# A perceiver layer: second-batch regrouping in its own buffer, most of it issued by SyncE, and the cross-attention's values one block sooner

## The chip, the cores and the metric

The kernel runs on one core of a Trainium2 chip. The metric is the device time of one execution in microseconds (us); the time before is the median of three runs, 1431.88 us (1429.88 to 1434.81). The engines are named as in the profile: PE (TensorE), ACT (ScalarE), DVE (VectorE), POOL (GpSimd) and SP (SyncE, which issues DMA transfers). ACT issues DMA transfers too; ACTq and SPq are the issues of the two.

## The reference

One layer of a perceiver, all in float32, for x of 2 x 256 tokens of width 256 and a context of 2 x 4096 tokens.

```python
x = x + xattn(layernorm(x), ctx, ctx)       # 16 heads of 64; softmax over 4096 keys
x = x + attn(layernorm(x))                  # self-attention, below
x = x + ffn(layernorm(x))                   # gated, weights in 4 bits, activations in 16

def attn(x):                                # k, v = 16 memory tokens + 256 own tokens
    dots = einsum('bhid,bhjd->bhij', q, k) * scale
    dots = einsum('bhij,hk->bkij', dots, pre_proj)      # heads are mixed ahead of the softmax
    dots = where(causal, finfo.min, dots)
    attn = softmax(dots)
    attn = einsum('bhij,hk->bkij', attn, post_proj)     # and behind it
    return (attn @ v) @ Wo
```

## The kernel before

Three stages follow one another: `cross_attention`, `self_attention`, `gated_ffn`. In each, every engine has a program of its own, written out by hand, and the engines meet by semaphores; an instruction waits for what is named ahead of it, and everything behind it on its engine waits too. The order of the lines is the order on the engine.

**Cross-attention.** 16 passes: 2 batches times 8 pairs of heads (`it` counts passes, `i` pairs in a batch). The 4096 keys are taken in 8 blocks of 512 (`STEPS`, index `j`). In the first half of a pass PE (`body`, L628) projects the keys of a block (`project_k`, L530) and, two blocks later, makes scores for the row maxima (`scores_for_max`, L559) in four score banks, which DVE reduces (L447) before the next block's scores overwrite them. Between them PE does what is left of the pass before (`sum_over_keys`, the denominators, after the scores of block 0; `project_output`, after those of block 2) and the value projections (`project_v`, L538): number j - 5 behind block j > 4, number 3 ahead of the last scores, 4 to 6 behind them, 7 after the transposes of the negated maxima (L655). DVE divides by the denominators (`divide`, L422) after the maxima of block 0 and adds the output to x (`add_output`, L430) after those of block 2. ACT copies keys and values out of the banks (`copy_v`, L352). Values alternate between two banks, `out_ps` (shared with denominators and output) and `v_ps` (shared with the queries); `v_bank` says which has the even ones. In the second half of a pass scores are made again, ACT takes exponentials, and PE multiplies by the values. In pair 0 of a batch each block has two value projections, one for each half of the keys.

**Self-attention.** Queries, keys and values are projected, and the dots of a pair of heads come out of PE with a query per partition. The head mix needs heads and 8 query rows together on the partitions (16 x 8 = 128), so the dots are regrouped by DMA from `dots_sb` to `grouped`: for each head one transfer for the near half (the first 128 queries, `t` = 0, 144 keys) and one for the far half (`t` = 1, 272 keys), each from 128 partitions to 8 (`send_dots`, L924). 16 heads, two halves and two batches make 64 transfers. Then 17 steps for each batch (`SA_STEPS`; n = 0 to 33) go through a pipeline: PE `mix(n)` (L1264), DVE mask and maximum, ACT exponentials, DVE reciprocals, POOL scales the second mixing matrix, PE `post(n - 3)` (L1277), DVE and ACT copy the result. Mix 0 and 17 wait for the near transfers of their batch, mix 8 and 25 for the far ones. Into the steps are woven: the transposes of the FFN's weights (steps 1 to 6, three banks in turn), the second batch's dots (`dots(PAIRS + u)`, steps 8 to 15, near and far of one pair at a time in one pair of banks), at step 20 the products of the first batch with its values (`all_products(0)`), and from step 22 its output projection.

The near and the far buffer of `grouped` exist once, for both batches. So SP and ACT send the second batch's near transfers only after 8 mixes are done, and the far ones after 17 (L953, L1082); SP sends the odd pairs of heads, ACT the even ones. A wait for the transfers of the memory values and of `v_last_b1` (the second batch's last 16 values, moved to the first partitions) stands ahead of mix 0 (L1352).

Of the kernel before, what the change touches and what calls it, by code (L numbers as in the profile page):

```python
# [12 lines left out]
P = 128  # L13
BATCH, SEQ, D = 2, 256, 256
# [63 lines left out]
def cross_attention(nc, x, ctx_in, w_q, w_k, w_v, w_o, x_res, ident):  # L78
# [16 lines left out]
    with ExitStack() as stack:  # L95
# [103 lines left out]
        def v_bank(m):  # L199
            return (out_ps, v_ps)[m % 2]  # L200
# [140 lines left out]
        def _(act):  # L341
# [20 lines left out]
            def body(it, b, i, parity):  # L362
# [5 lines left out]
                for j in range(STEPS + 1):  # L368
# [13 lines left out]
                    if j > 4:  # L382
                        copy_v(b, i, parity, j - 5)
                for j in range(STEPS - 4, STEPS - 1):
                    copy_v(b, i, parity, j)
# [32 lines left out]
        def _(dve):  # L418
# [17 lines left out]
            def body(it, b, i, parity):  # L436
# [7 lines left out]
                for j in range(STEPS):  # L444
# [4 lines left out]
                    if j == 0 and it > 0:  # L449
                        divide(it - 1)  # L450
# [43 lines left out]
        def _(pe):  # L494
# [43 lines left out]
            def project_v(it, b, i, parity, j):  # L538
# [89 lines left out]
            def body(it, b, i, parity):  # L628
                if not opened_before(it):
                    open_pair(it, b, i)  # L630
                for j in range(2, STEPS):
# [12 lines left out]
                    if j > 4:  # L644
# [5 lines left out]
                for j in range(STEPS - 4, STEPS - 1):  # L650
                    project_v(it, b, i, parity, j)
# [111 lines left out]
def self_attention(nc, w_q, w_kv, w_o, pre_proj, post_proj, mem_k, mem_v, w_gate, w_up, hidden_wT,  # L763
                   x_res, ident):

    with ExitStack() as stack:
# [26 lines left out]
        v_last_b1 = r.sbuf("v_last_b1", [MEM, INNER])  # L793
# [47 lines left out]
        dots_copied = [r.sem("dots_by_act"), r.sem("dots_by_dve")]  # L841
        regrouped = [r.sem("regrouped_near"), r.sem("regrouped_far")]
# [24 lines left out]
        def dots_bank(u):  # L867

            return pair_bank[u % 2 if u < PAIRS else 0]

        def hidden_bank(m):
            return bank[m % 3]
# [46 lines left out]
        DOTS_AT = SA_STEPS // 2  # L919
        HIDDEN_AT = 1  # L920
# [3 lines left out]
        def send_dots(eng, b, pair, t):  # L924

            for h in (2 * pair, 2 * pair + 1):
                eng.dma_start(grouped[t][h * ROWS:(h + 1) * ROWS, :, :], dots_sb[t][:, h, :]
# [5 lines left out]
        def _(sp):  # L933
# [16 lines left out]
            sp.dma_start(v_last_b1[:, :], v_last[MEM:2 * MEM, :]).then_inc(last_in, 16)  # L950
# [55 lines left out]
        def copy_dots(eng, scaled_copy, u):  # L1006

            pair = u % PAIRS
            eng.wait_ge(dots_made, u + 1)
            if u >= PAIRS:  # L1010
                for t in range(QT):
                    eng.wait_ge(regrouped[t], ALL_REGROUPED)
            src = dots_bank(u)
            scaled_copy(dots_sb[0][:, 2 * pair:2 * pair + 2, :], src[:, :, 0:NEAR])
            scaled_copy(dots_sb[1][:, 2 * pair:2 * pair + 2, :], src[:, :, NEAR:NEAR + KEYS]
                        ).then_inc(dots_copied[u % 2], 1)

        @block.scalar
        def _(act):
# [10 lines left out]
            def send(b, pair):  # L1030

                act.wait_ge(dots_copied[0], (b * PAIRS + pair) // 2 + 1)
                for t in range(QT):
                    send_dots(act, b, pair, t)
# [32 lines left out]
            for n in range(STEP_ALL + LAG):  # L1067
# [4 lines left out]
                if HIDDEN_AT <= n - 1 < HIDDEN_AT + 2 * WT_BANKS:  # L1072
                    m = n - 1 - HIDDEN_AT
                    act.wait_ge(hidden_made, m + 1)
                    copy(hidden_wT[:, m // WT_BANKS, m % WT_BANKS * 512:(m % WT_BANKS + 1) * 512], hidden_bank(m)
                         ).then_inc(hidden_copied, 1)
                u = n - DOTS_AT
                if 0 <= u < PAIRS and u % 2 == 0:
# [653 lines left out]
```

## Time and profile before

| | |
|---|---|
| median of 3 runs | 1431.88 us (1429.88 to 1434.81) |
| profiled execution | 1433.27 us, its span 1431.1 us |
| busy in the span | PE 1262.2 us (88%), DVE 877.0 (61%), ACT 723.9 (51%), POOL 412.6 (29%) |
| mean granted PE clock | 0.952 of full speed |
| cross-attention, self-attention, FFN | until about 1125, until about 1337, until 1431 |

All times in rows are microseconds from the start of the span. Busy time is the time of an engine's instructions, without its waits. A line of code can have several groups of instructions, as it makes different tiles. A row of a timeline has an instruction or a run of equal ones; in square brackets stands how long the engine had been idle before it, and what it then waited for.

### The profile page before, as it was taken

To read this page: it belongs to the slowest core of one execution; us is meant where nothing else is said; L and a number is where in the kernel's file an instruction comes from. 1 tells how busy PE (TensorE), PEld (TensorE's weight loads), DVE (VectorE), ACT (ScalarE), POOL (GpSimd) and SP (SyncE) were. 2 spreads that over 40 slices of the span, in tenths; PEclk is the share of its full clock that TensorE was granted. 3 is DMA by queue.
4 is the path that set the end of the run, shared out by engine and by line. 5 is a ranking of instruction groups with operands and counts; after the bars stand their busy time and mean duration, and the time that the engine had idled before them with its cause. 6 is when DMAs were issued, how large, how long until landed. Compare 5 with 4: busy or idle time off the path is not lost. (4 is left out here: it accounts for less than half of the span.)

```text
span 1431.1 us, 21060 instructions
## 1 busy us (share of the span) xinstructions
PE 1262.2 (88%) x8379; PEld 943.1 (66%) x8379; DVE 877.0 (61%) x1042; ACT 723.9 (51%) x1304; POOL 412.6 (29%) x372
## 2 busy tenths in 40 slices
PE   3999999999999999899999999999999697569643
PEld 2786877768686868586868687776868344346322
DVE  4647666676766676647676766667676456304476
ACT  3655656565555555545565565656554133214153
POOL 3605051432425150414251505143241103102000
PEclk9999999999999999999999999999999799859876
DMA  4203020203111132211121303030311442330000
GB/s 150 74 1 78 1 78 1 78 1 78 30 49 49 27 84 83 77 30 30 49 52 27 78 1 78 0 78 1 74 31 33 164 61 41 48 49 1 22 0 15
DMA packets 42528, 68.19 MB, mean 48 GB/s; under 512 B 5040, under 2 KB 31152, under 8 KB 42432
## 3 DMA queue, kind: packets, MB, share of 16 engines
q1 hardware_dynamic: 37632, 63.39, 17.1%
q10 hardware_dynamic: 4800, 3.48, 1.9%
q8 instruction: 66, 1.08, 0.3%
q14 instruction: 30, 0.25, 0.1%
HBM read 25.89 MB, written 0.52 MB: 18 GB/s over the span
## 5 line engine op out<-in xcount | busy, mean ns | idle before, releaser
L447 DVE TENSOR_REDUCE step_max<-score_banks 128x2 f32<-128x1024 f32 x256 | 299.0, 1220 | 124.3 <-PE score_banks L571 124.3
L468 DVE TENSOR_TENSOR prob_sum<-prob_sum,probs 128x1024 f32<-128x1024 f32 x224 | 279.3, 1288 | 139.6 <-ACT probs L398 138.9
L330 POOL TENSOR_TENSOR k_split<-probs,k_split 64x512 fp32r<-64x512 f32 x128 | 163.4, 1277 | 328.8 <-ACT probs L381 323.8
L398 ACT ACTIVATE probs<-score_banks 128x1024 f32<-128x1024 f32 x181 | 181.9, 1028 | 149.3 <-PE out_ps L597 85.3
L585 PE MATMUL score_banks<-q_twice,k_split 128*128 128x256 f32 x724 | 182.2, 288 | 0.2 <-ACT probs L398 0.2
L586 PE MATMUL score_banks<-q_low_max,k_ones 128*128 128x256 f32 x724 | 178.1, 283 | 0.0
L332 POOL TENSOR_TENSOR k_split<-probs,k_split 64x512 fp32r<-64x512 f32 x128 | 164.0, 1281 | 9.6
L585 PEld LDWEIGHTS score_banks<-q_twice,k_split 128*128 128x128 f32 x724 | 138.3, 191 | 11.9 <-issue 6.2
L323 POOL TENSOR_TENSOR w_lo<-w_raw,w_hi 128x768 fp32r<-128x768 f32 x16 | 36.2, 2261 | 355.5 <-ACT w_hi L349 355.5
L586 PEld LDWEIGHTS score_banks<-q_low_max,k_ones 128*128 128x128 f32 x724 | 138.5, 191 | 0.0
L373 ACT ACTIVATE k_split<-key_banks 64x512 fp32r<-64x512 f32 x128 | 75.6, 590 | 119.2 <-PE key_banks L534 118.6
L571 PE MATMUL score_banks<-k_split,q_twice 64*128 64x512 f32 x512 | 103.3, 461 | 27.9 <-DVE step_max L447 27.9
L597 PE MATMUL out_ps<-probs,v_near 128*64 128x256 f32 x1024 | 121.0, 383 | 0.4 <-ACT probs L398 0.4
L597 PE MATMUL out_ps<-probs,v_far 128*64 128x256 f32 x1024 | 120.9, 383 | 0.0
L398 ACT ACTIVATE probs<-key_banks 128x1024 f32<-128x1024 f32 x75 | 77.1, 1029 | 43.7 <-PE out_ps L597 42.9
L534 PE MATMUL key_banks<-ctxT_lo,w_hi 128*128 128x512 f32 x256 | 93.1, 445 | 2.6 <-ACT probs L381 1.4
L597 PEld LDWEIGHTS out_ps<-probs,v_near 128*64 128x64 f32 x1024 | 69.8, 137 | 38.8 <-issue 2.4
L597 PEld LDWEIGHTS out_ps<-probs,v_far 128*64 128x64 f32 x1024 | 69.9, 137 | 38.4 <-issue 2.9
L571 PEld LDWEIGHTS score_banks<-k_split,q_twice 64*128 64x128 f32 x512 | 42.4, 186 | 79.1 <-issue 30.5
L534 PE MATMUL key_banks<-ctxT_hi,w_lo 128*128 128x512 f32 x256 | 81.8, 401 | 0.0
L534 PE MATMUL key_banks<-ctxT_hi,w_hi 128*128 128x512 f32 x256 | 81.6, 400 | 0.0
L381 ACT ACTIVATE probs<-key_banks 128x512 f32<-128x512 f32 x128 | 76.7, 599 | 4.8 <-POOL k_split L332 1.7
(207 smaller groups left out, 2204.4 us busy)
## 6 DMA issues: line engine op xcount, KB each, us to landing
k_ones<-k_split SPq DMA_DIRECT2D x128, 256.0 KB, 4.0
ctx_rows<-in_ctx_dram SPq DMA_DIRECT2D x10, 512.0 KB, 3.8
w_raw<-in_L_xattn_w_v_dram SPq DMA_DIRECT2D x14, 256.0 KB, 3.5
probs<-in_ctx_dram SPq DMA_DIRECT2D x6, 512.0 KB, 6.2
grouped_far<-dots_far ACTq DMA_DIRECT2D x16, 136.0 KB
grouped_far<-dots_far SPq DMA_DIRECT2D x16, 136.0 KB
w_raw<-in_L_xattn_w_q_dram SPq DMA_DIRECT2D x16, 128.0 KB, 3.6
w_raw<-in_L_xattn_w_k_dram SPq DMA_DIRECT2D x16, 128.0 KB, 3.5
```

The lines of the kernel that those rows point to most:

```text
L330: pool.tensor_tensor(k_split[DH:P, A, keys], keys_staged[j % 2][0:DH], k_split[0:DH, A, keys].bitcast(F32), ALU.subtract).then_inc(k_low[A ...
L332: pool.tensor_tensor(k_split[0:DH, B, keys], keys_staged[j % 2][DH:P], k_split[DH:P, B, keys].bitcast(F32), ALU.subtract).then_inc(k_low[B ...
L373: act.activation(k_split[0:DH, A, keys], ps[0:DH, :], ACT.Copy).then_inc(k_high, 1)
L381: act.activation(keys_staged[j % 2], ps[:, :], ACT.Copy).then_inc(k_staged, 1)
L398: act.activation(probs[:, j % 2, h, :], scores_of, ACT.Exp, scale=SCALE).then_inc(exp_done, 1)
L447: dve.tensor_reduce(step_max[:, qt, :, j], score_banks[:, 2 * qt:2 * qt + 2, :], X, ALU.max).then_inc(max_done, 1)
L468: dve.tensor_tensor(prob_sum[:, h, :], prob_sum[:, h, :], probs[:, j % 2, h, :], ALU.add).then_inc(sum_done, 1)
L534: last = mm(k_ps[j % 2][:, :], w[:, c, 0:PAIR], s[:, c, j * CHUNK:(j + 1) * CHUNK], start=(n == 0), stop=(n == len(passes) - 1))
L571: last = mm(score_banks[:, 2 * qt + 1 - h, :], q_twice[rows, h, qt * P:(qt + 1) * P], k_split[rows, h, keys], start=True, stop=True)
L585: mm(out, k_split[:, h, keys], q_twice[:, h, :], start=True, stop=False)
L586: last = mm(out, k_ones[:, h, keys], q_low_max[:, h, :], start=False, stop=True)
L597: last = mm(out_ps[h * DH:(h + 1) * DH, SEQ:2 * SEQ], v[:, h * DH:(h + 1) * DH], probs[:, j % 2, h, t * SEQ:(t + 1) * SEQ], start=(j == 0 ...
```

## The change

Cross-attention:
- In pairs with i > 0 the value projections stand behind the blocks 3, 5, 6 and 7 (numbers 0 to 3), one is put ahead of the last scores (4) and two behind them (5, 6). In pair 0 of a batch they stay.
- Even values take `v_ps`, odd ones `out_ps`, and the two waits for these banks change places.
- DVE divides after the maxima of block 1 (before: block 0).

Self-attention:
- `grouped` has a near buffer for each batch; the far one is still shared. `v_last_b1` lies in `xnT`, which is no longer needed by then.
- The second batch's dots are split: the near ones of pair n are made in step n (0 to 7) in the first pair of banks, the far ones in steps 8 to 15 in the same banks. ACT and DVE copy them by turns, each at its own step; PE makes the next pair's when the last one's copy is done.
- The second batch's near transfers are issued by SP as soon as a pair is copied; its far ones all by SP, after 17 mixes. Of the first batch ACT issues the near transfers of even pairs, SP all others.
- The FFN's weight transposes stand in steps 1, 3, 5, 7, 9 and 11, in one bank.
- The waits for the memory values and `v_last_b1` go from ahead of mix 0 to the products of the first batch.

```diff
 # cross-attention
         def v_bank(m):
-            return (out_ps, v_ps)[m % 2]
+            return (v_ps, out_ps)[m % 2]
+        def values_behind(i, j):
+            return (j - 5 if j > 4 else None) if i == 0 else {3: 0, 5: 1, 6: 2, 7: 3}.get(j)
+        def values_left(i):
+            return list(range(3 if i == 0 else 4, STEPS - 1))
...
-                    if j == 0 and it > 0:
+                    if j == 1 and it > 0:
                         divide(it - 1)
...
                     if t == 0 and m == 0:
+                        pe.wait_ge(q_low, 2 * it + 2)
+                    elif t == 0 and m == 1:
                         wait_past(pe, y_added, it)
-                    elif t == 0 and m == 1:
-                        pe.wait_ge(q_low, 2 * it + 2)
...
-                    if j > 4:
-                        project_v(it, b, i, parity, j - 5)
+                    if values_behind(i, j) is not None:
+                        project_v(it, b, i, parity, values_behind(i, j))
                 scores_for_max(it, STEPS - 2)
-                project_v(it, b, i, parity, STEPS - 5)
+                project_v(it, b, i, parity, values_left(i)[0])
                 scores_for_max(it, STEPS - 1)
-                for j in range(STEPS - 4, STEPS - 1):
+                for j in values_left(i)[1:]:
                     project_v(it, b, i, parity, j)
 # self-attention: buffers and SP's program
-        grouped = [r.sbuf("grouped_near", [P, P // ROWS, NEAR]), r.sbuf("grouped_far", [P, P // ROWS, KEYS])]
+        near = [r.sbuf(f"grouped_near{b}", [P, P // ROWS, NEAR]) for b in range(BATCH)]
+        far = r.sbuf("grouped_far", [P, P // ROWS, KEYS])
+        grouped = [[near[b], far] for b in range(BATCH)]
...
-            for pair in range(1, PAIRS, 2):
-                sp.wait_ge(dots_copied[1], pair // 2 + 1)
-                for t in range(QT):
-                    send_dots(sp, 0, pair, t)
+            for pair in range(PAIRS):
+                sp.wait_ge(dots_copied[pair % 2], pair // 2 + 1)
+                if pair % 2 == 1:
+                    send_dots(sp, 0, pair, 0)
+                send_dots(sp, 0, pair, 1)
+            for pair in range(PAIRS):
+                sp.wait_ge(near_copied[pair % 2], pair // 2 + 1)
+                send_dots(sp, 1, pair, 0)
...
-            for t in range(QT):
-                sp.wait_ge(mix_made, SA_STEPS // 2 if t == 0 else SA_STEPS)
-                for pair in range(1, PAIRS, 2):
-                    sp.wait_ge(dots_copied[1], PAIRS // 2 + pair // 2 + 1)
-                    send_dots(sp, 1, pair, t)
+            sp.wait_ge(mix_made, SA_STEPS)
+            for pair in range(PAIRS):
+                sp.wait_ge(far_copied[pair % 2], pair // 2 + 1)
+                send_dots(sp, 1, pair, 1)
 # ACT and DVE, in step n (ACT parity 0, DVE parity 1)
+        def second_dots(eng, scaled_copy, n, parity):
+            if n < PAIRS and n % 2 == parity:
+                copy_near(eng, scaled_copy, n)
+            if FAR_AT <= n < FAR_AT + PAIRS and (n - FAR_AT) % 2 == parity:
+                copy_far(eng, scaled_copy, n - FAR_AT)
...
-                if n == DOTS_AT + PAIRS or n == SA_STEPS + 1:
-                    t = 0 if n == DOTS_AT + PAIRS else 1
-                    act.wait_ge(mix_made, SA_STEPS // 2 if t == 0 else SA_STEPS)
-                    act.wait_ge(dots_copied[0], PAIRS)
-                    for pair in range(0, PAIRS, 2):
-                        send_dots(act, 1, pair, t)
 # PE
+            def near_dots(pair):
+                if pair > 0:
+                    pe.wait_ge(near_copied[(pair - 1) % 2], (pair - 1) // 2 + 1)
+                pair_dots(1, pair, 0, pair_bank[0]).then_inc(near_made, 1)
+            def far_dots(pair):
+                if pair == 0:
+                    pe.wait_ge(near_copied[(PAIRS - 1) % 2], PAIRS // 2)
+                else:
+                    pe.wait_ge(far_copied[(pair - 1) % 2], (pair - 1) // 2 + 1)
+                pair_dots(1, pair, 1, pair_bank[0]).then_inc(far_made, 1)
...
-                if HIDDEN_AT <= n < HIDDEN_AT + 2 * WT_BANKS:
-                    transpose_hidden(n - HIDDEN_AT)
-                if DOTS_AT <= n < DOTS_AT + PAIRS:
-                    dots(PAIRS + n - DOTS_AT)
+                if hidden_at(n) is not None:
+                    transpose_hidden(hidden_at(n))
+                if n < PAIRS:
+                    near_dots(n)
+                if FAR_AT <= n < FAR_AT + PAIRS:
+                    far_dots(n - FAR_AT)
```

## Rows read from the trace of the kernel before

**Rows 1.** PE's waits, whole span: line, waited for: us, times, longest.
```profile
PE score_banks L571 <- DVE step_max L447: 27.9, 46, 1.1
PE bank L1273 <- DMA grouped_near<-dots_near: 25.3, 1, 25.3
...
PE bank L1311 <- ACT mixed_last L1021: 4.3, 1, 4.3
```
**Rows 2.** PE's timeline in one pass: start, us, line, tiles, count, idle before.
```profile
665.49 0.73 PE L571 MATMUL score_banks<-k_split,q_twice 64*128 64x512 f32 x4
...
668.33 0.72 PE L571 MATMUL score_banks<-k_split,q_twice 64*128 64x512 f32 x4
668.99 0.73 PE L534 MATMUL key_banks<-ctxT_lo,w_hi 128*128 128x512 f32 x2
...
671.79 0.49 PE L571 MATMUL score_banks<-k_split,q_twice 64*128 64x512 f32 x2 [1.14 <-DVE step_max L447]
672.83 0.50 PE L571 MATMUL score_banks<-k_split,q_twice 64*128 64x512 f32 x2 [0.54 <-DVE step_max L447]
673.26 1.13 PE L614 MATMUL out_ps<-wo_pair,outT 128*128 128x256 f32 x4
...
676.38 0.51 PE L554 MATMUL out_ps<-w_hi,ctxT_lo 128*128 128x256 f32 x2
...
677.92 0.62 PE L534 MATMUL key_banks<-ctxT_lo,w_hi 128*128 128x512 f32 x2
...
693.16 0.38 PE L655 MATMUL key_banks<-ident,neg_max 128*128 128x128 f32 x2
```
**Rows 3.** DVE's timeline in the same pass.
```profile
666.03 2.36 DVE L447 TENSOR_REDUCE step_max<-score_banks 128x2 f32<-128x1024 f32 x2 [3.21 <-PE score_banks L571]
668.31 1.75 DVE L425 RECIPROCAL prob_sum<-out_ps 128x256 f32<-128x256 f32 x1
...
670.43 4.61 DVE L447 TENSOR_REDUCE step_max<-score_banks 128x2 f32<-128x1024 f32 x4
...
691.24 0.17 DVE L456 TENSOR_SCALAR neg_max<-row_max 128x4 f32<-128x4 f32 x1
```
**Rows 4.** PE's timeline in the self-attention: mixes 0, 16, 17, 25, first second-batch dots.
```profile
1197.30 0.95 PE L1273 MATMUL bank<-grouped_near,kron 128*128 128x64 f32 x4 [4.88 <-DMA v_last_b<-v_last]
...
1213.29 0.97 PE L1260 MATMUL bank<-kT,qT 64*128 64x144 f32 x8
...
1233.58 0.73 PE L1273 MATMUL bank<-grouped_far,kron 128*128 128x272 f32 x2
...
1260.48 0.69 PE L1273 MATMUL bank<-grouped_near,kron 128*128 128x64 f32 x2 [25.29 <-DMA grouped_near<-dots_near]
...
1295.03 0.70 PE L1273 MATMUL bank<-grouped_far,kron 128*128 128x320 f32 x2
```
**Rows 5.** Windows: length, busy PE, PEld, DVE, ACT, POOL; PE clock, DMA share, GB/s.
```profile
1213.00:1235.00 22.00, 21.71 (x143) 14.17 (x141) 13.17 (x41) 12.09 (x45) 4.91 (x8) 1.00 0.10 21
...
1260.00:1267.00 7.00, 6.49 (x28) 5.28 (x28) 2.81 (x14) 1.87 (x10) 1.63 (x3) 0.59 0.13 24
1271.00:1286.00 15.00, 14.69 (x96) 8.41 (x96) 0.00 (x0) 2.74 (x8) 0.00 (x0) 0.50 0.45 48
...
1318.00:1329.00 11.00, 9.55 (x103) 6.21 (x104) 0.68 (x3) 3.45 (x11) 0.00 (x0) 1.00 0.01 2
...
1236.00:1259.00 23.00, 0.00 (x0) 0.00 (x0) 0.00 (x0) 0.50 (x2) 0.00 (x0) 0.55 0.57 80
1265.25:1283.00 17.75, 13.41 (x86) 7.93 (x86) 1.83 (x9) 4.07 (x17) 1.23 (x2) 0.60 0.56 64
```
**Rows 6.** DVE's timeline: the mask of mix 0.
```profile
1201.28 0.19 DVE L1152 TENSOR_TENSOR bank<-bank,causal 128x32 f32<-128x32 f32 x1
```
**Rows 7.** ACT's timeline: its first far transfer of the second batch.
```profile
1263.99 0.62 ACTq L927 DMA_DIRECT2D grouped_far<-dots_far  x1
```
**Rows 8.** DMA issues, whole span: tiles, queue, count, size of each.
```profile
grouped_far<-dots_far ACTq DMA_DIRECT2D x16, 136.0 KB
```

More of the change, by code:

```diff
@@ L381, in body @@
                         act.activation(keys_staged[j % 2], ps[:, :], ACT.Copy).then_inc(k_staged, 1)
-                    if j > 4:
-                        copy_v(b, i, parity, j - 5)
-                for j in range(STEPS - 4, STEPS - 1):
+                    if j < STEPS and values_behind(i, j) is not None:
+                        copy_v(b, i, parity, values_behind(i, j))
+                for j in values_left(i):
                     copy_v(b, i, parity, j)
@@ L865, in projection_bank, with dots_bank, hidden_at @@
             return bank[4 + n % 4]
[L867 to L872, printed above, removed]
+        def dots_bank(pair):
+            return pair_bank[pair % 2]
+        def hidden_at(n):
+            return n // 2 if n > 0 and n % 2 == 1 and n // 2 < 2 * WT_BANKS else None
         def mix_bank(n):
@@ L1032, in send @@
                 act.wait_ge(dots_copied[0], (b * PAIRS + pair) // 2 + 1)
-                for t in range(QT):
-                    send_dots(act, b, pair, t)
+                send_dots(act, b, pair, 0)
             def exponentials(n):
@@ L1243, in project, with pair_dots, first_dots @@
                 last.then_inc(proj_made, 1)
-            def dots(u):
-                b, pair = u // PAIRS, u % PAIRS
-                if u < PAIRS:
-                    for eng in range(2):
-                        pe.wait_ge(proj_copied[eng], pair + 1)
-                if u == PAIRS:
-                    pe.wait_ge(hidden_copied, 2 * WT_BANKS)
-                back = 2 if u < PAIRS else 1
-                if u >= back:
-                    pe.wait_ge(dots_copied[(u - back) % 2], (u - back) // 2 + 1)
-                for t in range(QT):
-                    at, keys = (0, NEAR)[t], dots_keys(t)
-                    tokens = slice((b * QT + t) * P, (b * QT + t + 1) * P)
-                    for half in range(2):
-                        rows = slice(half * DH, (half + 1) * DH)
-                        last = mm(dots_bank(u)[:, half, at:at + keys], qT[rows, pair, tokens], kT[rows, pair, b, 0:keys],
-                                  start=True, stop=True)
-                last.then_inc(dots_made, 1)
+            def pair_dots(b, pair, t, out):
+                tokens = slice((b * QT + t) * P, (b * QT + t + 1) * P)
+                for half in range(2):
+                    rows = slice(half * DH, (half + 1) * DH)
+                    last = mm(out[:, half, 0:dots_keys(t)], qT[rows, pair, tokens], kT[rows, pair, b, 0:dots_keys(t)],
+                              start=True, stop=True)
+                return last
+            def first_dots(pair):
+                for eng in range(2):
+                    pe.wait_ge(proj_copied[eng], pair + 1)
+                if pair >= 2:
+                    pe.wait_ge(dots_copied[pair % 2], pair // 2)
+                pair_dots(0, pair, 0, dots_bank(pair))
+                pair_dots(0, pair, 1, dots_bank(pair)[:, :, NEAR:]).then_inc(dots_made, 1)
+            def near_dots(pair):
[8 more added lines that the diff above has]
+                pair_dots(1, pair, 1, pair_bank[0]).then_inc(far_made, 1)
             def mix(n):
@@ L1273, in mix @@
                 mm(mix_bank(n)[:, 0:count * keys].rearrange("p (g c) -> p g c", g=count),
-                   kron[:, 0, :, :].rearrange("p k r -> p (k r)"), grouped[t][:, first:first + count, 0:keys],
+                   kron[:, 0, :, :].rearrange("p k r -> p (k r)"), grouped[b][t][:, first:first + count, 0:keys],
                    start=True, stop=True).then_inc(mix_made, 1)
@@ L1294, in transpose_hidden @@
                 pe.wait_ge(hidden_chain, (w + 1) * W_OPS)
-                if m >= 3:
-                    pe.wait_ge(hidden_copied, m - 2)
+                wait_past(pe, hidden_copied, m)
                 for k in range(4):
-                    last = transpose_weight(pe, hidden_w[w], FC, at * 4 + k, hidden_bank(m)[:, k * P:(k + 1) * P], ident)
+                    last = transpose_weight(pe, hidden_w[w], FC, at * 4 + k, bank[2][:, k * P:(k + 1) * P], ident)
                 last.then_inc(hidden_made, 1)
@@ L1315, in all_products @@
             def all_products(b):
-                for eng in range(2):
-                    pe.wait_ge(dots_copied[eng], PAIRS)
+                if b == 0:
+                    for eng in range(2):
+                        pe.wait_ge(far_copied[eng], PAIRS // 2)
+                    pe.wait_ge(memv_in, 32)
+                    pe.wait_ge(last_in, 16)
+                    pe.wait_ge(hidden_copied, 2 * WT_BANKS)
                 wait_past(pe, y_added, b * QT)
@@ L1341, in _ @@
                 if pair > 0:
-                    dots(pair - 1)
+                    first_dots(pair - 1)
             project(NQK)
-            dots(PAIRS - 1)
+            first_dots(PAIRS - 1)
             for n in range(NQK + 1, NPROJ):
```

53 lines of the change are left out of this document (27 added, 26 removed).

## The prediction

> **What bounds the kernel now.** I read the waits of TensorE (PE) first: [rows 1] name the stretches in which the busiest engine (1262 of 1431 us) stands still. Two bear on this change: 27.9 us in 46 waits of the cross-attention's scores (L571) for the running maxima of VectorE (DVE, L447), and one wait of 25.3 us of the self-attention's mixing product (L1273) for the near regrouping transfers of the second batch. The timelines of PE and DVE over one pair of heads [rows 2, 3] show where the first arises: DVE takes the maxima of block 0, then divides the pair before (668.31 to 670.43), and only then the maxima of block 1. The scores of block 2 overwrite the banks of block 1, so PE waits 1.14 and 0.54 us at 671.79 and 672.83. The second is the hole between mix 16 at 1233.58 and mix 17 at 1260.48 [rows 4]: the second batch's near dots may leave only when mix 7 and the copies are done, into the buffer that the first batch used, and ACT's half of them is issued from 1235 on, beside the far half of SP. The windows [rows 5] give the rate of these transfers and the clock before and after the hole.
>
> **The cross-attention, step by step.** The trace has 16 passes over a pair. In the 14 with i > 0, one value projection goes from behind the scores of block 7 to behind those of block 1, and the divide goes behind the maxima of block 1. No instruction is added.
> Removed: PE was ready for the scores of block 2 at 671.79 - 1.14 = 670.65 and got to the output projection (L614) at 673.26, 2.61 us for work that takes 0.66 undisturbed (668.33 to 668.99) [rows 2]. That is 1.95 us lost a pair.
> What is late next: the maxima of block 1 start 0.54 us after the scores, as those of block 0 do (665.49 to 666.03), at 668.9, and take 2.28 (666.03 to 668.31); the divide takes 2.12 [rows 3], so outT is there at 673.3. PE does the moved values (1.54, 676.38 to 677.92), the keys of block 4 (670.65 - 668.99 = 1.66) and the scores of block 2 (0.66) from 668.99 on, and is at L614 at 672.85. It waits there some 0.6, with the hand-over of 0.1 that the waits show. Then the transposes of the maxima (693.16) have one value projection less ahead of them; the negated maxima end at 691.41 [rows 2, 3], a slack of 1.75 that the earlier arrival eats without exceeding it (691.41 + 0.2 against 691.96). Gain: 1.95 - 0.7 = 1.25, of which I take 1.2, nearest to these rows. Bounds: 0 if the output projection loses as much as the scores did, 1.95 if nothing waits.
> 14 x 1.2 = 16.8. Pass 8 (i = 0, second batch) has no value projection to move in, only the later divide: its output projection comes at best when it does now, -0.2. The values' swap of banks costs nothing: the first now waits for the low queries (DVE makes them ahead of its first maxima and had been idle for 3.21 us at 666.03 [rows 3]), the second for the added output, one step later. Sum: -16.6, bounds 0 to -27.
>
> **The start of the self-attention's steps.** PE's wait of 4.88 us for v_last_b1 ahead of mix 0, at 1197.30 [rows 4], goes to the products of the first batch, where its transfer is long done. It brings 0: DVE, which quantises weights until then, masks mix 0 only at 1201.28 [rows 6], 4 us after PE's wait ended. The first batch's regrouping goes to SP's queue for all far and half of the near transfers; ACT keeps 8 near ones. These 32 transfers had landed, the near ones at least, by 1197.30; in another order over the same DMA engines the near ones have until 1201 and the far ones until mix 8, 1212. I count 0; if the far queue of SP is late, it shows as a wait of mix 8.
>
> **Steps 0 to 16.** A pair of second-batch dots (0.97 us on PE [rows 4]) was issued in each step 8 to 15; now the near part (144 of 416 keys, 0.34) is in steps 0 to 7, the far part where both were. Steps 8 to 15 last 2.9 us each, (1233.58 - 1213.29) / 7, with PE busy 21.71 of 22 us [rows 4, 5], so 8 x 0.34 = 2.7 come off. Added in steps 0 to 7: one near bank is used by turns, so PE waits in each step for the copy of the step before, which stands on ACT behind the exponentials and the hidden-weight copy, and the mix behind waits too. The trace shows no such wait; 0 if it falls into PE's early idle time, 5 us if each step lasts 0.6 longer. I take 2.3, the middle. Mix 16 then stands at 1233.2, within 2.5.
>
> **Mix 17.** The near transfers of the second batch go into their own buffer as soon as each pair is copied, from about 1203 to 1216, with two of 72 KB per step and nothing beside them. They land before 1225. So 25.3 goes, and the far ones are late next.
>
> **The far transfers.** SP sends all 16 after mix 16 (it waits for all 17 mixes, as the buffer is shared), from about 1233.7. Each is 136 KB [rows 8]. The nearest row: eight of them alone on ACT's queue, first issue 1263.99 [rows 7], kept the DMA engines at an even share from 1265.25 to 1283, 17.7 us or 2.2 each, at 64 GB/s [rows 5]. So 1.3 + 16 x 2.2 = 36.7 us: landing at 1270.4. PE would need them at mix 25: now 1295.03 - 1260.48 = 34.6 us after mix 17 [rows 4]; of this, 6.5 go because the products, 15 us at a granted clock of 0.50 [rows 5], ran in 8.5 at 1.00 in the window of 1318, 2.5 of the 4.3 us before them go with the far issues on ACT [rows 1], and 1.2 with steps 17 to 19 at full clock. That leaves 24.4, so PE arrives at about 1259 and waits 11 to 12 us. The wait of 25.3 becomes one of half its length: mix 25 at 1270.4, 24.6 earlier.
> Bounds: 16 transfers at the 80 GB/s of two queues together [rows 5] need 28 us (mix 25 at 1263); at 2.7 each, with near ones beside, 43 (1278).
> After such a wait the clock is low: after 1260.48 it granted 0.59 over 7 us [rows 5], that is, 5.7 us at half (1.2 GHz) before the full 2.4. Busy PE loses half of that, 2.9; I take +2.5, bounds 0 and 8. Sum: -22.1, bounds -14 to -36.
>
> Here the Trainium skill bears on it (DMA: Bandwidth & Descriptors, "Issuing engines are not separate DMA queues"): transfers issued on several engines end on the same DMA engines, and more issuing engines save only issue time. By that, SP alone would keep the 80 GB/s of two queues, and the sum would be 7 us lower; the row of ACT alone has 64, and I go by the row.
>
> **Sum.** The profiled execution took 1433.27 us (span 1431.1 and 2.2 around it), 1.4 above the median of the three runs. 1433.3 - 16.6 - 22.1 = 1394.6; as a median, 1393.
>
> **Rivals.**
> (A) The forecast, 1393: the far transfers become the wait. For it: 2.2 us each, evenly, in the only stretch where they run alone. Chance 0.60.
> (B) One queue keeps the rate of two: mix 25 at 1263, 1386. For it: in [rows 5] both queues together moved 80 GB/s; against it, 64 alone. 0.15.
> (C) The far transfers are in time (94 GB/s and more): no wait and no low clock, -36 in the self-attention, 1379. Against it, no row shows such a rate for them. 0.08. The Trainium skill (DMA: Bandwidth & Descriptors, "Specifications") gives some 27 GiB/s per DMA engine; with the half of sixteen that the share shows, an estimate is 10 us for all far transfers, which is this case; the 64 GB/s of this trace speaks against it.
> (D) The cross-attention gains nothing: the output projection, or the transposes of the maxima, wait as long as the scores did. Price: 16.6 back, 1410. For it: the divide now ends 0.5 after PE gets there, and the slack at the transposes is used up. 0.11.
> (E) Slower: steps 0 to 7 in turns with the copies leave PE short pauses, and the clock falls to half there and stays. PE's 21.7 busy us of 1213 to 1235 double, with some 5 before them: mix 16 at 1260, far landing at 1297, 2 later than mix 25 now; then the 42 us from mix 25 to the stage's end, with PE busy 9.55 of 11 us in the window of 1318, grow by 36: +38, less 16.6, 1453. It decides once steps 8 to 15 last 4.5 us and the clock stays at 0.5. For it: between 1271 and 1286 the clock stayed at 0.50 with PE busy 14.69 of 15 us; against it, it was 1.00 in 1213 to 1235 after a start at less [rows 5]. 0.04. The skill has that rule (TensorE: Matmul & The Clock Gate, "A second HAM failure mode: psum-queue depth-cycling"): short idle times between groups of matmuls let the clock swing between its levels.
> 0.02 is left for what I don't see.
>
> **How the numbers follow.** What a measurement tells from no change is 0.3%, 4 us. A to D are all faster: 0.94; E slower, 0.04; same 0.02. A's own range is 1385 to 1402: 5 us from the far rate, 2.5 from mix 16, 5 from the pairs. With B, most of C and some of D: 1380 to 1406.
>
> **What would show it.** Right: L571's wait for L447 falls from 27.9 to below 8, L614 gets one of 0.5 to 0.8 in each of 14 pairs, the pair's period falls by 1.2; mix 17 has no wait for near transfers; mix 25 waits 8 to 16 us for grouped_far, at half clock behind it. Wrong: a wait at L655 for neg_max of over 0.3, mix 16 after 1237 less the 17 us of the pairs, a wait of mix 17, or none of mix 25.

## The result, and the profile after

The changed kernel takes 1400.4 us (median of 4 runs, 1398.7 to 1401.0) against 1433.4 for the kernel before beside it: a ratio of 0.9767, interval 0.9737 to 0.9797. The forecast was 1393 within 1380 to 1406, so the time came out faster, as forecast, 7 us above the point. The profiled execution took 1400.91 us (span 1398.7), 32.4 less span than before. The first transposes of the self-attention split this: they start at 1132.02 us before and at 1110.48 after, 21.5 us sooner where 16.6 was forecast. The self-attention, from them to its last output projection, gave 12.0 where 22.1 was forecast: 196.75 us before (1328.77 - 1132.02) and 184.73 after (1295.21 - 1110.48). What is behind it is 1.2 longer (in the traces of all kernels here it takes 102.3 to 105.6 us). Both terms were mis-sized, in opposite directions.

PE's waits in the changed kernel, which answer to [rows 1] (us in total, times, longest):
```profile
PE out_ps L622 <- DVE outT L436: 13.5, 16, 2.3
...
PE bank L1304 <- DMA grouped_far<-dots_far: 11.1, 1, 11.1
...
PE bank L1271 <- ACT dots_near L1056: 7.6, 1, 7.6
...
PE score_banks L579 <- DVE step_max L455: 3.1, 17, 0.3
```
The scores' wait for the maxima went from 27.9 to 3.1 us, and the output projection has one of 13.5 in its place, of which the 2.3 behind the last pass were there before too. The wait for near transfers is gone and one of 11.1 for far transfers is there. The 7.6 us for a near copy had no place in the prediction.

PE's timeline in the pass of [rows 2]. The values (L562) follow the scores of block 1, the scores of block 2 have no wait, and the output projection (L622) waits 0.68:
```profile
657.14 0.72 PE L579 MATMUL score_banks<-k_split,q_twice 64*128 64x512 f32 x4
657.79 0.50 PE L562 MATMUL v_ps<-w_hi,ctxT_lo 128*128 128x256 f32 x2
...
660.80 0.73 PE L579 MATMUL score_banks<-k_split,q_twice 64*128 64x512 f32 x4
662.21 1.13 PE L622 MATMUL out_ps<-wo_pair,outT 128*128 128x256 f32 x4 [0.68 <-DVE outT L436]
```
PE's timeline in the self-attention, answering to [rows 4]: the first transposes, the first mixes and near dots, mixes 8, 16, 17 and 25.
```profile
1110.48 1.75 PE L1226 MATMUL bank<-ident,outT 128*128 128x128 f32 x7 [6.68 <-DVE outT L64]
...
1172.15 0.41 PE L1304 MATMUL bank<-grouped_near,kron 128*128 128x64 f32 x2 [1.28 <-DMA grouped_near<-dots_near]
1172.49 0.52 PE L1271 MATMUL bank<-kT,qT 64*128 64x144 f32 x4
...
1181.48 0.85 PE L1271 MATMUL bank<-kT,qT 64*128 64x144 f32 x4 [7.64 <-ACT dots_near L1056]
...
1197.77 0.81 PE L1304 MATMUL bank<-grouped_far,kron 128*128 128x320 f32 x2
...
1218.82 0.73 PE L1304 MATMUL bank<-grouped_far,kron 128*128 128x272 f32 x2
...
1220.26 0.33 PE L1304 MATMUL bank<-grouped_near,kron 128*128 128x64 f32 x2
...
1259.25 1.43 PE L1304 MATMUL bank<-grouped_far,kron 128*128 128x320 f32 x2 [11.10 <-DMA grouped_far<-dots_far]
```
Counted from the first transposes, mix 16 stands at 108.3 us; in the kernel before it was 101.6. Mix 17 follows without a wait. Mix 25 comes 40.4 us after mix 16, in place of 61.5.

Windows of the changed kernel, columns as in [rows 5] (length; busy PE, PEld, DVE, ACT, POOL; PE's granted clock, DMA share, GB/s): the start of the steps, the end of the near dots, and what follows mix 25.
```profile
1176.00:1180.00 4.00, 0.00 (x0) 0.00 (x0) 3.93 (x4) 0.00 (x0) 0.41 (x1) 0.50 0.00 0
1180.00:1184.00 4.00, 2.52 (x11) 1.75 (x12) 1.89 (x10) 1.86 (x12) 0.85 (x2) 0.50 0.15 34
1184.00:1188.00 4.00, 4.00 (x16) 2.52 (x16) 1.05 (x4) 1.86 (x9) 0.99 (x2) 0.50 0.58 67
1188.00:1192.00 4.00, 4.00 (x16) 2.36 (x14) 1.29 (x7) 1.80 (x8) 0.61 (x1) 0.50 0.31 47
1192.00:1196.00 4.00, 3.90 (x22) 2.43 (x20) 1.53 (x7) 1.68 (x9) 1.23 (x2) 0.87 0.23 53
...
1259.00:1264.00 5.00, 4.75 (x12) 3.68 (x13) 1.08 (x4) 0.86 (x4) 0.61 (x1) 0.50 0.00 0
```
PE stood still until 1181 and then worked at half its clock (0.50, that is 1.2 GHz) for 12 us (until 1193); in 1184 to 1192 it was busy without a gap, so these steps were bound by PE at half speed.

### The profile page after: what moved, and what is told of

The parts are those of the page before. It is cut to its first block and busy times, and to the rows that moved or that the text cites. A ratio compares the mean times of both kernels' runs of the same rounds, so it can differ in the third digit from the quotient of the medians.

```text
span 1398.7 us, 21065 instructions
## 1 busy us (share of the span) xinstructions
PE 1257.7 (90%) x8379; PEld 939.1 (67%) x8379; DVE 879.3 (63%) x1042; ACT 723.3 (52%) x1304; POOL 411.8 (29%) x372
## 5 line engine op out<-in xcount | busy, mean ns | idle before, releaser
L381 ACT ACTIVATE k_split<-key_banks 64x512 fp32r<-64x512 f32 x128 | 75.5, 590 | 104.7 <-PE key_banks L542 104.1
L579 PE MATMUL score_banks<-k_split,q_twice 64*128 64x512 f32 x512 | 98.9, 453 | 3.1 <-DVE step_max L455 3.1
L542 PE MATMUL key_banks<-ctxT_hi,w_hi 128*128 128x512 f32 x256 | 80.7, 396 | 0.0
L382 ACT ACTIVATE k_split<-key_banks 64x512 fp32r<-64x512 f32 x128 | 75.8, 593 | 3.1
```

Of the source, the lines that this page charges most:

```text
L382: act.activation(k_split[DH:P, B, keys], ps[DH:P, :], ACT.Copy).then_inc(k_high, 1)
L542: last = mm(k_ps[j % 2][:, :], w[:, c, 0:PAIR], s[:, c, j * CHUNK:(j + 1) * CHUNK], start=(n == 0), stop=(n == len(passes) - 1))
L579: last = mm(score_banks[:, 2 * qt + 1 - h, :], q_twice[rows, h, qt * P:(qt + 1) * P], k_split[rows, h, keys], start=True, stop=True)
```

## The experiments

Each ran on the chip beside the kernel before; times are medians, intervals those of the ratio to it. "Rel." is the time from the first transposes of the self-attention.

**One part alone.** Two kernels: the changed cross-attention with the old self-attention, and the reverse.

> The cross-attention edits alone; self-attention is that of the kernel before. Theory (the gain of the two parts adds up, as the two traces read: first transposes of self-attention 21.5 us sooner, of which 11 passes of some 1.24 us and three stretches at half clock that the changed kernel does not have): 1432 - 21.5 = about 1411 us, and the trace has at most one stretch at clock 0.50 between 100 and 1050 us. Rival (the stretches at half clock come and go from one execution to the next, and only the predicted 16.6 us belong to the edits): 1415 to 1417, and other executions differ from each other by 1.6 us and its multiples.

> The self-attention edits alone; cross-attention is that of the kernel before. Theory (the parts add up; steps 0 to 16 lost 6.8 us by the turn-taking of TensorE and the copies of the near dots, and 25.3 us of waiting went): 1432 - 11 = about 1421 us, mix 8 some 87 us and mix 16 some 108 us after the first transposes, as in the changed kernel. Rival (the slow start of the steps comes from what cross-attention left behind, a later landing of the first near transfers or the clock): mix 16 some 102 us after the first transposes as before, and 1413 to 1416 us.

Measured: 1409.5 us [0.9825, 0.9858] and 1421.9 us [0.9902, 0.9944]. The gains, 22.8 and 10.4, add up to 33.1, against 33.0 for both. The cross-attention alone has one stretch at half clock (586 to 590 us), as the changed kernel has at 585 to 589. The kernel before has three:
```profile
190.00:192.00 2.00, 2.00 (x8) 0.64 0.05 15
192.00:194.00 2.00, 2.00 (x8) 0.50 0.85 267
...
454.00:456.00 2.00, 2.00 (x5) 0.50 0.55 158
...
870.00:872.00 2.00, 2.00 (x6) 0.50 0.12 30
```
(Length, busy PE, its clock, DMA share, GB/s.) The self-attention alone, whose cross-attention is the old one, has four (from 387, 581, 598 and 871 us). So they do come at different places in each execution, as the rival has it, but three and four with the old waits stand against one and one with the new. Over all kernels of this document the three with the old waits show 3, 4 and 4, the eleven with the values moved 0 to 2. A pass with such a stretch takes some 1.6 us longer (66.9 against 65.3 in the kernel before). In its steps the self-attention alone has mix 16 at rel. 105.8, between what theory (108) and rival (102) gave (the run with the values alone, below, has 105.8 too); mix 25 waits 14.9 us.

**One edit of the cross-attention alone** (self-attention as changed). In the first kernel the values go back, and with them their number ahead of the last scores, their banks and the waits for these (not shown):
```
-  return (j - 5 if j > 4 else None) if i == 0 else {3: 0, 5: 1, 6: 2, 7: 3}.get(j)
+  return j - 5 if j > 4 else None
```
In the second the division goes back:
```
-  if j == 1 and it > 0: divide(it - 1)
+  if j == 0 and it > 0: divide(it - 1)
```


> The changed kernel with the value projection and its banks put back; only the division stands one step later in cross-attention. Theory (the projection of values behind the scores of step 1 is what fills the gap that TensorE had before the scores of step 2): the gap is only moved on by a step, most of the 1.2 us a pass is lost again, 1412 to 1419 us. Rival (the place of the division matters, the maximum of step 1 is no longer behind it): 1400 to 1406 us.

> The changed kernel with the division of cross-attention put back behind the first maxima; the value projection stays sooner. Theory (the values fill the gap): 1400 to 1406 us, with a wait of the scores of step 2 for the maxima that is shorter than the 1.7 us a pass of the kernel before by one group of value products. Rival (the place of the division matters): 1412 to 1419 us.

Measured: 1425.4 [0.9933, 0.9971] and 1397.4 [0.9741, 0.9798]. PE's waits with the division moved only:
```profile
PE out_ps L622 <- DVE outT L436: 26.6, 16, 2.3
```
and with the values moved only:
```profile
PE score_banks L579 <- DVE step_max L455: 9.2, 32, 1.1
```
Without the values, the later division moves the wait from the scores (27.9 us before, 5.9 left) to the output projection (2.3 before), nearly whole, and nothing is gained over the self-attention alone (1421.9); the 1425.4 lie beyond the 1412 to 1419 of the theory too. The values alone give as much as both. That confirms the theory. The division's new place gains nothing: the 3 us against it (1397.4 to 1400.4) are within the intervals of the medians, but the traces show a small cost in each pass. The denominators of two passes that follow each other, in the changed kernel and, below, with the values alone:
```profile
244.67 0.65 PE L614 MATMUL out_ps<-prob_sum,ones 128*64 128x256 f32 x4
308.74 0.65 PE L614 MATMUL out_ps<-prob_sum,ones 128*64 128x256 f32 x4
```
```profile
244.60 0.65 PE L614 MATMUL out_ps<-prob_sum,ones 128*64 128x256 f32 x4
308.53 0.65 PE L614 MATMUL out_ps<-prob_sum,ones 128*64 128x256 f32 x4
```
A pass takes 64.07 us there and 63.93 here. In the traces of this kernel and of the three further ones with the values moved and the division in its old place it is 63.9 in all undisturbed passes, in those with both moved 64.0 to 64.1, and the output projection's 0.68 us are there only with the division moved. So the later division costs 0.1 us a pass, some 2 us over 14.

**Later near dots.** Near dots in steps 3 to 10, far dots in 11 to 18:
```
-  FAR_AT = SA_STEPS // 2
+  NEAR_AT = 3
+  FAR_AT = 11
```


> The changed kernel with the second batch's near dots in steps 3 to 10 in place of 0 to 7, and its far dots in 11 to 18 in place of 8 to 15. Theory (the changed kernel lost 6.8 us in steps 0 to 16 because the near dots of step 1 wait for a copy behind the first exponentials, 7.64 us, and TensorE then works at half clock until the middle of the steps): without that wait mixes 0 to 2 and the first hidden transposes run ahead, mix 16 comes 102 to 105 us after the first transposes of self-attention in place of 108.3, and the time falls by 3 to 6 us, to 1394 to 1397. Rival (each step lasts as long as the turn of dots and copies, wherever it begins): mix 16 at 107 to 109 and 1399 to 1402 us. In both the far transfers still begin after mix 16 and PE waits 9 to 12 us for them before mix 25.

Measured: 1398.8 [0.9723, 0.9792], not to be told from the changed kernel. Mix 16 stands at rel. 104.5, as the theory has it, but PE waits 7.9 us ahead of mix 3 all the same, now for the exponentials of step 0, which are behind VectorE's quantising; so the premise of the theory, no such wait, failed, and the time missed its 1394 to 1397 us. Against the 105.8 of the kernels with the changed kernel's self-attention mix 16 gained only 1.3 us, and these shrink into the wait at mix 25 (12.7 us).

**Copies ahead of the exponentials and maxima:**
```
+  second_dots(act, scaled_copy, n, 0)
   if n < STEP_ALL: exponentials(n)
   ...
-  second_dots(act, scaled_copy, n, 0)
```
(and the same on VectorE, ahead of its maximum).

> The changed kernel with the copy of the second batch's dots of each step ahead of that step's exponentials (ScalarE) or maxima (VectorE), no longer behind them. Theory (turn-taking: TensorE's dots of one step wait for a copy that stands behind the exponentials of the step before): the 7.64 us wait is cut to some 3 to 6, since VectorE, which quantises weights until about 69 us after the first transposes, still holds the second copy; mix 16 at 104 to 107 us in place of 108.3, the time 1396 to 1400. Rival (the lost time is the half clock alone, which any wait of this length brings): mix 16 at 108, 1400.

Measured: 1410.8 [0.9813, 0.9877], 10 us slower than the changed kernel, which neither theory nor rival had. The first half of the theory held: in place of 7.64 us PE waits 2.97 and 2.32 for the near copies. But mix 16 came at rel. 116.7: steps 8 to 16 took 31.3 us, not 21.1. Timelines of ACT and DVE in step 9 and 10 (start, us, line, tiles, idle before):
```profile
1209.35 0.62 ACT L1056 ACTIVATE dots_far<-bank 128x544 f32<-128x544 f32 x1 [1.55 <-PE bank L1271]
1209.87 0.41 ACT L1074 ACTIVATE expd<-bank,neg_top 128x192 f32<-128x192 f32 x1
```
```profile
1213.68 0.72 DVE L1166 TENSOR_SCALAR dots_far<-bank 128x544 f32<-128x544 f32 x1 [5.64 <-PE bank L1271]
1214.33 0.19 DVE L1175 TENSOR_TENSOR bank<-bank,causal 128x32 f32<-128x32 f32 x1
```
PE's dots stand last in its step, so a copy put first on ACT or DVE holds the step's own exponentials and maxima until PE has finished the step. Before, these ran ahead of it.

**A far buffer of its own** for the second batch, laid over fields that are dead after step 11 (`v_last_b1`, which lay in one of them, moves to `qT`; shortened):
```
+  second_far = r.sbuf("second_far", [P, P // ROWS * KEYS])   # weights, scales, tokens
+  far = [r.sbuf("grouped_far", ...), second_far]
...
-  sp.wait_ge(mix_made, SA_STEPS)
+  sp.wait_ge(hidden_made, 2 * WT_BANKS)
```


> The changed kernel with a far buffer of its own for the second batch, laid over the quantised weights, their scales and the normalised tokens, which nothing reads after step 11; SyncE sends each far pair when it is copied and the hidden transposes are done, no longer after mix 16. Theory (the far transfers' late start is what sets mix 25): they begin some 13 us sooner, the wait of 11.1 us before mix 25 falls to 0 to 2, and part of the half clock behind it (2.2 us) goes: 1387 to 1391 us. Rival (transfers at some 60 GB/s beside the steps slow or hold the steps back, or the products of the first batch are late next): a new wait takes 5 us or more of it back, 1393 to 1398.

Measured: 1385.5 [0.9638, 0.9699]. SP issues the far transfers from 1207.7 us on; PE's mix 25 and, below it, the window in which they run:
```profile
1246.53 0.81 PE L1307 MATMUL bank<-second_far,kron 128*128 128x320 f32 x2 [0.58 <-ACT shared L1056]
```
```profile
1210.00:1244.00 34.00, 29.92 (x214) 0.95 0.57 61
```
The wait is 0.58 us and for something else; mix 25 comes 27.4 us after mix 16. The transfers keep the rate (61 GB/s) that they had alone, and the steps beside them are not slower: steps 8 to 16 take 21.1 us in both. The late start of the far transfers is what the changed kernel waited for. From mix 25 to the last output projection it takes 33.5 us, not 36.0, so the half clock behind the wait went with it.

**Far transfers over two queues,** half of them issued by ACT (shortened):
```
-  for pair in range(PAIRS): sp.wait_ge(far_copied[...]); send_dots(sp, 1, pair, 1)
+  for pair in range(1, PAIRS, 2): ...send_dots(sp, 1, pair, 1)
+  if n == SA_STEPS + 1: for pair in range(0, PAIRS, 2): send_dots(act, 1, pair, 1)
```


> The changed kernel with the second batch's far transfers after mix 16 split evenly over the queues of SyncE and ScalarE. Theory (the transfers themselves set the rate, 2.36 us each at a DMA share near 0.58, whichever engine issues them): they land at the same time within 2 us, mix 25 still waits 9 to 12 us, 1398 to 1404. Rival (two queues keep more in flight, the 80 GB/s that the kernel before had in its stretch of 23 us): 27 us in place of 37.7, the wait falls to 0 to 2 us, 1389 to 1393.

Measured: 1400.5 [0.9736, 0.9812], no gain; but not for the theory's reason. The DMA engines were busy with them from 1222.9 to 1254.0, 31 us in place of the 36.5 of one queue. Three windows (length, busy PE, its clock, DMA share, GB/s):
```profile
1225.00:1235.00 10.00, 2.50 (x15) 0.71 0.58 62
1236.00:1242.00 6.00, 2.01 (x14) 0.50 0.58 110
1243.00:1253.00 10.00, 10.00 (x68) 0.50 0.57 61
```
Until 1235 only SP's transfers moved, from 1242 on only ACT's, each at the rate of one queue (61 and 62 GB/s). In the 7 us between both moved, at 110. So two queues do add up; the gain is small because ACT's, though issued from 1225.4 on, moved so late. No run shows why. And ACT paid for it, and with it PE:
```profile
1225.44 0.65 ACTq L940 DMA_DIRECT2D grouped_far<-dots_far  x1
...
1226.77 11.10 ACTq L940 DMA_DIRECT2D grouped_far<-dots_far  x6
1237.98 0.31 ACT L1074 ACTIVATE expd<-bank,neg_top 128x64 f32<-128x64 f32 x1 [11.39 <-issue]
```
```profile
1239.99 1.60 PE L1346 MATMUL bank<-shared,v_sb 128*64 128x256 f32 x8 [11.83 <-ACT mixed_last L1053]
```
Behind two issues of 0.65 us, the next six took 1.85 each. The exponentials behind them and the products of the first batch waited 11 us, as long as the wait at mix 25 that went, and PE was at half clock for 27 us. Two queues without ACT were not tried. The Trainium skill (DMA: Bandwidth & Descriptors, "Issuing engines are not separate DMA queues") holds that more issuing engines save only issue time; this trace does not agree: with two queues at work the same kind of transfer ran at 110 GB/s, with one at 61 and 62.

**Putting together.** The far buffer with the division put back, and then the later dots as well:

> The second far buffer and the division put back behind the first maxima, both against the changed kernel. Theory (the value projection carries the whole gain of cross-attention, the later division only moves its wait to the output projection, and the two parts add up): 1381 to 1386 us, mix 16 to mix 25 some 27 us as with the far buffer alone. Rival (the division's place is worth its part of the 1.2 us a pass): 1388 us or more.

> As the run before, and the second batch's near dots in steps 3 to 10, its far dots in steps 11 to 18. Theory (the steps that lose time are those where near dots meet the half clock; the far transfers, 38 us from step 11 on, still land before mix 25): mix 16 at 103 to 105 us after the first transposes, mix 25 with a wait of at most 2 us, 1379 to 1384 us, 2 to 3 under the run before. Rival (the far dots, three steps later, make the far transfers late, or the products of the first batch wait for them): a wait of 4 us or more at mix 25 or ahead of the products, 1384 to 1390.

Measured: 1386.7 [0.9659, 0.9700] and 1382.0 [0.9632, 0.9681]. The division put back adds nothing measurable to the far buffer (1385.5), though its passes are the 0.1 us shorter here too (63.9 against 64.1). With later dots mix 16 stands at rel. 104.3 and mix 25 has no wait. This version beats both kernels: its interval ends at 0.9681, that of the changed kernel begins at 0.9737. Whether it beats the far buffer alone is open, as the intervals overlap.

**No near dots** (the second batch's near dots and their copies are left out, and the first batch's are sent in their place, each pair when the mix of the step behind it is done; shortened):
```
-  if n < PAIRS: near_dots(n)
...
-  if n < PAIRS and n % 2 == parity: copy_near(eng, scaled_copy, n)
```


> The changed kernel without the second batch's near dots and their copies (what is sent in their place is the first batch's); all transfers stay, each near pair leaves when the mix of the step behind it is done. Theory (the near dots and their turn with the copies are what steps 0 to 16 lost): mix 16 at 100 to 102.5 us after the first transposes, as in the kernel before (101.6) or sooner; since the far transfers start from there, the time falls by 4 to 7 us, to 1393 to 1396. Rival (the hidden transposes, now in one bank and in every other step, or the length of the half clock, lost it): mix 16 at 104.5 or later, 1398 or more.

Measured: 1395.4 [0.9721, 0.9752]; mix 8 at rel. 80.7 (changed kernel 87.3, before 80.1) and mix 16 at rel. 101.7, as the theory has it. The loss is that of the near dots in steps 0 to 7; steps 8 to 16 take 21.0 us with and without. The stretch at half clock in the steps lasted 10 us here, as it did in the self-attention alone and with the values alone, where mix 8 stands at 84.7: at the same length of it the near dots cost 4.0 us; the other 2.6 of the changed kernel came with its 17 us.

**The clearing of the mixed scores on ACT** in place of POOL, on top of the best version (in short; ACT and DVE wait for the clears only where the fields are first written):
```
-  pool.memset(mixed_first, 0.0); pool.memset(mixed_second, 0.0)
+  act.activation(mixed_first, mixed_first, ACT.Copy, scale=0.0)   # mixed_second after step 2
```


> As the run before last (second far buffer, later dots, division put back), and the two fields that collect the mixed scores are cleared by ScalarE, which idles there for 10.7 us, no longer by GpSimd: the second rounding pass of the weights on VectorE (128x1536) takes 5.70 us in the changed kernel, where GpSimd's two clears of 3.51 and 2.02 us run, and 0.95 where none does. Theory (that pass waits for the clears, and TensorE's wait of 7.6 to 7.9 us ahead of the steps waits for it): the pass takes 0.9 to 1.1 us, the mask of mix 0 comes 4 to 5 us sooner, the wait is 3 to 5 us, and the time is 1377 to 1380, 2 to 5 under that run. Rival (ScalarE's clear of 4096 columns holds back the first exponentials as long as the pass held the maxima, or the half clock is only met elsewhere): 1381 to 1384.

Measured: 1381.8 [0.9610, 0.9658], no difference to 1382.0. The timelines of DVE and POOL in the changed kernel, and of DVE here:
```profile
1171.52 5.70 DVE L756 TENSOR_SCALAR wide<-wide 128x1536 f32<-128x1536 f32 x1
```
```profile
1170.94 3.51 POOL L992 MEMSET shared<- 128x4096 f32 x1 [57.56 <-PE bank L1263]
1174.39 2.02 POOL L993 MEMSET shared<- 128x2304 f32 x1
```
```profile
1170.96 0.94 DVE L756 TENSOR_SCALAR second_far<-second_far 128x1536 f32<-128x1536 f32 x1
```
The theory's first half holds: the pass shrinks, and PE's wait falls from 7.9 to 1.7 us against the version it is built on (there this pass and the next took 3.74 and 2.73 us beside the clears). Its second half falls: mix 16 is at rel. 103.9, against 104.3. The half clock lasted from rel. 66 to 80, not 67 to 77, and a hidden transpose waited 1.9 us behind ACT's second clear. Behind mix 16 the two traces are not alike: the profiled execution here was the slowest of five (1386.7), with 17 us at half clock around the first batch's products, that of the best version the fastest (1379.5), with 3.

## Why the prediction was right or wrong, point by point

**Cross-attention: mechanism right, size off by 5 us.** The wait at the scores went, the output projection got one of 0.68, the pass became about 1.24 us shorter in 11 of the 14 passes; 1.2 was taken. The other three gained about 2.85: there the kernel before had run 1.6 us slower beside the half-clock stretches, which the term left out; how many of them an execution has is in part luck. Pass 8 lost 1.2, not 0.2, in the one stretch that is left. That the division had a share in the gain was implied by treating the two edits as one; the values carry it alone, and the division costs 0.1 us a pass. The step "what is late next" could have shown it, since the wait that it found at the output projection is there for the division alone.

**v_last and the first regrouping: right.** The wait of 4.88 us went and brought nothing; DVE's mask of mix 0 is at rel. 69.4 against 69.3.

**Steps 0 to 16: the step that failed.** Forecast -0.4, measured +6.8 (+4.2 in the two runs with the same code and a shorter half clock, the "twins"). In steps 0 to 7 I took +2.3 (as the middle of 0 and 5, which is 2.5) and wrote that "0 if it falls into PE's early idle time, 5 us if each step lasts 0.6 longer". The runs show +7.2 in the changed kernel, +4.6 in its twins, and +0.6 without near dots. Two things were missed: the second near dots wait for a copy behind DVE's quantising, so PE stood 7.64 us with mix 2 behind them, which the kernel before had made by then; and at half clock, in which rival E was priced only as a state that stays, each pair of near dots takes 0.85 us (0.52 at full clock, 1172.49), not the 0.34 of the sum, which had divided a pair by its keys. In steps 8 to 15 the forecast had -2.7 and measured -0.4. The far part and what follows it, in step 8:
```profile
1198.94 0.73 PE L1271 MATMUL bank<-kT,qT 64*128 64x272 f32 x4
1199.60 0.86 PE L1304 MATMUL bank<-grouped_far,kron 128*128 128x352 f32 x2
```
From start to start it takes 0.66 us, where the pair took 0.90 (1213.29 to 1214.19 before): 0.24 a step came off, not 0.34, so 1.9 in all. Two of the hidden transposes, which the sum did not count, moved into these steps and took 1.2 of it back. The sign set for this step, mix 16 after 1220, did not show (1218.8), but only because the cross-attention gave 21.5 us and not 17: that was luck.

**The near wait: right.** Gone; mix 17 follows mix 16 by 1.44 us.

**Far transfers: right, 3.2 us long.** PE waits 11.1, where 11 to 12 was forecast. From mix 16 to mix 25 it is 40.4, not 37.2: the DMA engines were done some 38 us after the first issue (forecast 36.7), and PE started some 1.6 us after that. The issues, and the last windows with a share (length, busy PE, clock, DMA share, GB/s):
```profile
1219.58 19.72 SPq L940 DMA_DIRECT2D grouped_far<-dots_far  x16
```
```profile
1222.00:1258.00 36.00, 23.40 (x160) 0.76 0.56 59
1257.00:1258.00 1.00, 0.00 (x0) 0.50 0.23 21
1258.00:1259.00 1.00, 0.00 (x0) 0.50 0.00 0
```
The choice of 64 GB/s over 80 was right for one queue (59). Rival B's premise, that one queue keeps the rate of two, fell with this and with the two-queue run (110 while both moved); C fell too, as it needed 94 GB/s of one. That the wait itself came out as forecast is in part luck: PE was 3.5 us late as well (29.3 us from mix 16 to its arrival, for 25.8), since the products of the first batch began at half clock.

**Half clock behind mix 25: right.** From mix 25 to the last output projection it takes 35.96 us against 33.74, so 2.2 for 2.5.

The sum: -21.5 for -16.6, -12.0 for -22.1, +1.2 for 0; it misses by 6.3, and the range held because the first two errors partly cancel.

What stays open: what sets the length of a half-clock stretch. In the same self-attention code it lasted 17 us in one execution (rel. 65.5 to 82.5), 10 in two others (66 to 76) and 20 with the division moved only (64 to 84), and mix 16 moved by 2.6 us with it (105.8 in the two, 108.3 and 108.4 in the others).

## What to carry to other kernels

Work pulled into an earlier loop step is to be priced at the clock and the idle time of that step, not where it came from, and its copies at the place in the queue where they stand: ahead of the step's own chain they cost 10 us more here than behind it. A shared buffer that delays a transfer was here better answered with dead storage than with a second queue: the second far buffer gave 15 us; the second queue gave none, as ACT, which issued on it, was held for 11. And where two edits are made as one, each is to be tried alone: here one carried the gain, and the other cost some 2 us.

## What was not expected of the hardware

- A DVE pass of 128x1536 took 5.70 us beside POOL's two clears (3.51 and 2.02 us) and 0.94 without them: it ended 0.8 us after the second clear, as if it had stood still until then. In the kernel before two such passes, of 3.74 and 2.73 us, ended 0.8 us after a clear each. The Trainium skill (SBUF — State Buffer, "SBUF: two separate sides") has a rule for it: VectorE and GpSimd share a pair of ports that one of them holds for a whole instruction. The trace agrees, with the 5.70 and 0.94 us; that the pass stood through two clears in one kernel and got in between them in the other, the rule does not say.
- Behind two of 0.65 us, six DMA issues on ACT took 1.85 us each while SP's transfers were under way; in the kernel before, six far ones on ACT alone took 3.89 us, 0.65 each. SP's sixteen alone took 19.72 us, 1.23 each.
- One queue moved the far transfers at 59 to 62 GB/s, two together at 110, at the same DMA share (0.56 to 0.58).
- In the cross-attention the clock fell to 0.50 for 3 to 4 us behind short waits, in some passes and not in others of the same shape: PE was busy for 2.3 of the 4 us before the fall at 190 us. The three kernels with the old waits show three to four such stretches, the eleven with the values moved none to two.
